# The slot lists of a mixture-of-experts router: loops written out, lanes dealt to three engines

## The chip, the cores and the metric

The kernel runs on one core of a Trainium2 chip. The metric is the device time of one execution in microseconds; the median of several executions is given. The profile is one more execution, taken with the hardware profiler.

## The reference

Input is `x` of shape (4, 2048, 256), so 8192 tokens of 256 numbers. One layer of causal attention with four heads is followed by a layer norm. Behind it stands a feed-forward layer with 32 experts and 16 adapters, and a second layer norm. Only the routing matters here:

```python
probs = softmax(h @ r2_w.T)                      # 8192 x 32
topp, topi = top_k(probs, 2)
wnorm = topp / topp.sum(-1, keepdims=True)       # the two gates of a token
score = where(routed, probs, -inf)
idx = argsort(-score, axis=0)[:cap].T            # cap = 320 tokens of each expert
w = take_along_axis(Wc.T, idx, 1) * valid        # their gates
```

Each expert works on at most 320 tokens. The kernel needs, for each expert and each of its slots, the token's number and its gate. The order of the slots within an expert is free, because the experts' outputs are added to the tokens' rows.

## The kernel before, in words

Four stages follow each other, each a block that ends with all engines meeting: `attention` (to about 1483 us of the span), `route` (to about 1786), `experts` (to about 2300) and `last_norm`.

In `route`, the 8192 tokens stand as 64 columns of 128 partitions. TensorE makes the logits, VectorE finds the two best experts of every token, searches each expert's threshold bit by bit (line 1214), and computes for each of the 64 x 2 pairs (token column, choice) the destination: a slot number from 0 to 12287, split into `dest_hi` (the slot's column, 0 to 95, since 32 experts have 3 columns of 128 slots each) and `dest_lo` (its lane, 0 to 127). Line 1274 releases the part that the change rewrites.

**The list stage** turns destinations into lists with matmuls. For each of the 128 pairs, `lane_hot` is a 128 x 128 matrix that has a 1 where the destination's lane is the column, and `col_hot` is a 128 x 192 matrix: 96 columns with the token's number plus 1 where the destination's column matches, and 96 with the gate there. The product of the two, added up over all 128 pairs in PSUM bank `ps[0]`, is the list: a slot that no pair hit stays 0. The pairs go in 16 lots of 8 (`LOT`, `LOTS`, lines 924 and 925), with two buffers, in a loop that handles two lots a turn:

- GpSimd (lines 1039 to 1051) waits until lot b - 2 is listed and ScalarE is through with it, copies the lot's 8 lane numbers to `lane_at` (1043), and makes the even lanes with a comparison (1046), four a lot.
- ScalarE (1069 to 1083) waits for that copy and makes the odd lanes, four a lot, each as an Abs (1076), a drain and a Relu (1078) of 1 - |distance|.
- VectorE (1277 to 1297) compares the column numbers for all 8 pairs at once (1282, 768 columns), drains, waits until lot b - 2 is listed, and multiplies by the token numbers (1289) and by the gates (1291).
- TensorE (1117 to 1135) waits for the columns of the lot, then for each lane in turn, and multiplies (1124). Its last matmul of the lot raises `listed`.

The buffers' release is what orders the engines: each of the three makers waits for `listed`. After the last lot VectorE reads PSUM (1299, 1300, 1302) and writes `slot_token` (1304) and `slot_weight` (1300). The block ends, and `experts` starts: GpSimd copies a list (1403) and gathers rows by it (1406). The weights of the first two experts were loaded in `route` (line 1006). Lines 801, 668 and 1658 are of the attention and of the last norm; they stand in the rows as instructions of the same kinds.

The waits, as TensorE has them:

```python
            def lists(b, r, first=False, last=False):
                pe.wait_ge(col_ready, b + 1)
                for n in range(LOT):
                    if n % 2:
                        pe.wait_ge(lane_odd, ODD + LOT // 2 * b + n // 2 + 1)
                    else:
                        pe.wait_ge(lane_even, LOT // 2 * b + n // 2 + 1)
```

Of the kernel before, what the change touches and what calls it, by code (L numbers as in the profile page):

```python
# [914 lines left out]
def route(nc, dram, NTT, cap, slot_token, slot_weight, w_raw, w_loaded):  # L915
# [8 lines left out]
    LOT = 8  # L924
    LOTS = NTT * TOPK // LOT
    assert TG % 4 == 0 and NTT % 16 == 0 and N <= 4096

    with ExitStack() as ctx:  # L928
# [25 lines left out]
        lane_hot = sb("lane_hot", [P, 2, LOT, P])  # L954
        lane_off = sb("lane_off", [P, 2, P])
        lane_at = sb("lane_at", [P, 2, LOT])
        col_eq = sb("col_eq", [P, 2, LOT, COLS])
        col_hot = sb("col_hot", [P, 2, LOT, 2, COLS])
        unit = sb("unit", [P, 1])
# [25 lines left out]
        dest_ready, lane_copied, lane_even, lane_odd = sem("dest_ready"), sem("lane_copied"), sem("lane_even"), sem("lane_odd")  # L985
        col_ready, listed = sem("col_ready"), sem("listed")

        LISTED, ODD = 2, LOT // 2 + 1

        def at(tensor, n, width=1):  # L990
            return tensor[:].rearrange("p a b c -> p (a b c)")[:, bass.ds(n, width)]
# [17 lines left out]
        def _(pool):  # L1009
# [24 lines left out]
            pool.sem_inc(lane_copied, ONE)  # L1034


            wait(pool, dest_ready, 1, pool_passed)

            def lanes(b, r):

                wait(pool, listed, LISTED + b - 1, pool_passed)
                wait(pool, lane_odd, ODD + (LOT // 2) * (b - 1), pool_passed)
                pool.tensor_copy(lane_at[:, r], at(dest_lo, LOT * b, LOT)).then_inc(lane_copied, 1)  # L1043
                wait(pool, lane_copied, ONE + b + 1, pool_passed)
                for n in range(0, LOT, 2):
                    pool.tensor_scalar(lane_hot[:, r, n, :], iota_p[:], lane_at[:, r, n:n + 1], None, ALU.is_equal)\
                        .then_inc(lane_even, 1)

            with pool.Fori(0, LOTS // 2) as j:
                for r in range(2):  # L1050
                    lanes(2 * j + r, r)
# [4 lines left out]
        def _(act):  # L1056
# [7 lines left out]
            act.sem_inc(lane_odd, ODD)  # L1064
# [4 lines left out]
            def lanes(b, r):  # L1069
                act.wait_ge(lane_copied, ONE + b + 1)  # L1070

                act.wait_ge(listed, LISTED + b - 1)
                for n in range(1, LOT, 2):

                    h = n // 2 % 2
                    act.activation(lane_off[:, h], iota_p[:], ACT.Abs, scale=-1.0, bias=lane_at[:, r, n:n + 1])  # L1076
                    act.drain()
                    act.activation(lane_hot[:, r, n, :], lane_off[:, h], ACT.Relu, scale=-1.0, bias=unit[:])\
                       .then_inc(lane_odd, 1)

            with act.Fori(0, LOTS // 2) as j:
                for r in range(2):
                    lanes(2 * j + r, r)

        @block.tensor
        def _(pe):
# [30 lines left out]
            def lists(b, r, first=False, last=False):  # L1117
                pe.wait_ge(col_ready, b + 1)
                for n in range(LOT):
                    if n % 2:  # L1120
                        pe.wait_ge(lane_odd, ODD + LOT // 2 * b + n // 2 + 1)
                    else:
                        pe.wait_ge(lane_even, LOT // 2 * b + n // 2 + 1)
                    mm = pe.matmul(ps[0][:, 0:2 * COLS], lane_hot[:, r, n, :], col_hot[:, r, n].rearrange("p a b -> p (a b)"),
                                   start=first and n == 0, stop=last and n == LOT - 1, skip_group_check=True)
                mm.then_inc(listed, 1)

            pe.sem_inc(listed, LISTED)
            lists(0, 0, first=True)
            lists(1, 1)  # L1130
            with pe.Fori(1, LOTS // 2 - 1) as j:
                for r in range(2):
                    lists(2 * j + r, r)
# [619 lines left out]
```

## Time and profile before

| | |
|---|---|
| median of 3 runs | 2359.52 us (2355.16 to 2361.84) |
| the profiled execution | 2361.54 us, its span 2359.6 us |
| mean granted clock of TensorE | 0.922 of full |
| TensorE matmul, busy | 1971.2 us (84%) |
| VectorE, busy | 1491.6 us (63%) |
| ScalarE, busy | 1331.8 us (56%) |
| GpSimd, busy | 823.7 us (35%) |
| GpSimd's lanes (line 1046), 64 of them | 64.7 us, 1028 ns each |
| from the start of line 1282 to that of line 1299 | 1712.14 to 1785.02 us |

How to read it: PE is TensorE's matmul, PEld its weight load, DVE VectorE, ACT ScalarE, POOL GpSimd. Times in the rows are microseconds from the span's start, unless ns is said. A float32 matmul is recorded as two weight loads and two matmuls. PEclk, in the table by stretches, is the granted clock, 1.0 being 2.4 GHz and 0.5 being 1.2 GHz. A timeline's row merges neighbouring instructions of one line and says how many (x4).

### The profile page before, as it was taken

To read this page: it belongs to the slowest core of one execution; us is meant where nothing else is said; L and a number is where in the kernel's file an instruction comes from. 1 tells how busy PE (TensorE), PEld (TensorE's weight loads), DVE (VectorE), ACT (ScalarE), POOL (GpSimd) and SP (SyncE) were. 2 spreads that over 40 slices of the span, in tenths; PEclk is the share of its full clock that TensorE was granted. 3 is DMA by queue.
4 is the path that set the end of the run, shared out by engine and by line. 5 is a ranking of instruction groups with operands and counts; after the bars stand their busy time and mean duration, and the time that the engine had idled before them with its cause. 6 is when DMAs were issued, how large, how long until landed. Compare 5 with 4: busy or idle time off the path is not lost. (4 is left out here: it accounts for less than half of the span.)

```text
span 2359.6 us, 43734 instructions
## 1 busy us (share of the span) xinstructions
PE 1971.2 (84%) x14340; PEld 1794.1 (76%) x14340; DVE 1491.6 (63%) x3318; ACT 1331.8 (56%) x3381; POOL 823.7 (35%) x937
## 2 busy tenths in 40 slices
PE   5799999999999999999999987501176999999990
PEld 5699988888988888988888876500155999999990
DVE  6655566656566656666666775288864666666655
ACT  4666665666665666665666653200065666666655
POOL 1122333333333333333111110000095666766652
PEclk9999999999999999999999998555598999999995
DMA  1000011001001001000000110300002444454428
GB/s 60 27 10 21 21 30 32 24 28 33 21 30 32 24 28 32 22 30 28 23 26 24 32 32 21 147 0 0 0 0 83 149 143 134 149 167 150 149 52 285
DMA packets 91405, 135.81 MB, mean 58 GB/s; under 512 B 16932, under 2 KB 79376, under 8 KB 87148
## 3 DMA queue, kind: packets, MB, share of 16 engines
q1 hardware_dynamic: 75372, 123.52, 15.2%
q0 software_dynamic: 15872, 10.24, 2.6%
q8 instruction: 90, 1.47, 0.3%
q14 instruction: 71, 0.58, 0.1%
HBM read 104.62 MB, written 39.85 MB: 61 GB/s over the span
## 5 line engine op out<-in xcount | busy, mean ns | idle before, releaser
L474 PE MATMUL out_ps<-v_sb,probs_t 128*128 128x64 f32 x4352 | 551.0, 271 | 17.6 <-DVE attn L773 15.1
L474 PEld LDWEIGHTS out_ps<-v_sb,probs_t 128*128 128x128 f32 x4352 | 532.4, 194 | 27.4 <-DVE probs_t L750 20.6
L736 DVE TENSOR_REDUCE part_max<-scores_ps 128x1 f32<-128x512 f32 (+3 forms) x576 | 356.9, 621 | 205.0 <-PE scores_ps L439 148.8
L611 ACT ACTIVATE probs<-scores_ps,neg_max 128x512 f32<-128x512 f32 (+3 forms) x640 | 398.1, 627 | 45.0 <-DVE neg_max L740 42.7
L439 PE MATMUL scores_ps<-k_st,q_parts 128*128 128x512 f32 (+3 forms) x1280 | 410.8, 403 | 11.4 <-ACT probs L611 5.0
L456 PE MATMUL probs_t_ps<-ident,probs 128*128 128x128 f32 x2176 | 347.6, 275 | 1.0 <-DVE probs_t L750 1.0
L620 ACT COPY probs_t<-probs_t_ps 128x512 f32<-128x512 f32 (+3 forms) x416 | 208.5, 501 | 244.6 <-PE probs_t_ps L456 243.2
L456 PEld LDWEIGHTS probs_t_ps<-ident,probs 128*128 128x128 f32 x2176 | 261.4, 142 | 51.4 <-issue 2.6
L1463 PE MATMUL up_ps<-xe_t,w 128*128 128x320 f32 x1920 | 288.9, 310 | 2.4 <-DVE xe_t L1570 1.7
L1463 PEld LDWEIGHTS up_ps<-xe_t,w 128*128 128x128 f32 x1920 | 283.6, 189 | 3.0 <-issue 1.9
L439 PEld LDWEIGHTS scores_ps<-k_st,q_parts 128*128 128x128 f32 x1280 | 200.5, 193 | 25.2 <-ACT probs L611 7.2
L879 POOL TENSOR_TENSOR rstd<-mean_var,power 128x1 f32<-128x1 f32 x64 | 35.6, 556 | 481.8 <-DVE mean_var L793 481.8
L898 POOL TENSOR_TENSOR products<-qk,cos_sin 128x256 f32<-128x256 f32 x176 | 125.4, 745 | 218.3 <-ACT qk L552 218.3
L1584 DVE SCALAR_TENSOR_TENSOR h<-silu,up_ps 128x320 f32<-128x320 f32 x160 | 77.1, 482 | 182.7 <-ACT silu L1540 182.7
L1426 POOL DMA_INDIRECT acc_rows<-out_rows,token x96 | 148.2, 1544 | 127.1 <-ACT out_rows L1553 116.1
L1463 PE MATMUL y_ps<-w,h_parts 128*128 128x256 f32 x1440 | 181.0, 285 | 0.0
L1463 PEld LDWEIGHTS y_ps<-w,h_parts 128*128 128x128 f32 x1440 | 174.4, 191 | 2.2
L1565 DVE TENSOR_TENSOR w<-w_raw,w 128x768 fp32r<-128x768 f32 x160 | 153.0, 958 | 5.0 <-ACT w L1518 0.7
L1406 POOL DMA_INDIRECT rows<-x_rows,token_in x96 | 129.8, 1352 | 48.3 <-POOL token_in L1403 27.5
L750 DVE COPY probs_t<-probs_t_ps 128x512 f32<-128x512 f32 (+1 forms) x224 | 145.9, 651 | 0.4 <-PE probs_t_ps L456 0.3
L1076 ACT ACTIVATE lane_off<-iota_p,lane_at 128x128 f32<-128x128 f32 x64 | 24.9, 390 | 206.6 <-POOL lane_at L1043 206.5
L1518 ACT CAST w<-w_raw 128x768 fp32r<-128x768 f32 x160 | 131.8, 826 | 2.0 <-PEq L928 2.0
(214 smaller groups left out, 3153.8 us busy)
## 6 DMA issues: line engine op xcount, KB each, us to landing
w_raw<-in_w_expert SPq DMA_DIRECT2D x32, 1536.0 KB, 6.4
w_raw<-in_w_adapter SPq DMA_DIRECT2D x32, 384.0 KB, 6.9
x_t<-in_x_t SPq DMA_DIRECT2D x64, 128.0 KB, 2.1
x_row<-in_x SPq DMA_DIRECT2D x64, 128.0 KB, 2.0
x_rows<-x SPq DMA_DIRECT2D x64, 128.0 KB, 1.7
acc_rows<-x SPq DMA_DIRECT2D x64, 128.0 KB, 1.8
ln_x<-acc_rows SPq DMA_DIRECT2D x16, 512.0 KB, 6.2
out_rows_dram<-ln_y SPq DMA_DIRECT2D x16, 512.0 KB, 5.2
```

What stands on the lines that cost most here:

```text
L439: mm = pe.matmul(out, q_parts[:, m % 2, part_, h, :], k_st[:, h, key_cols(g)], start=part_ == 0, stop=part_ == 1 and not diagonal)
L456: mm = pe.transpose(t_ps[:, g % 2, a:a + P], probs[:, g % PROBS_RING, a:a + P], ident[:])
L474: mm = pe.matmul(o_ps[:, h, :], probs_t[:, g % PT_RING, a - lo:a - lo + P], v_sb[:, slot(b, a // P), h, :], start=a == 0, stop=a == t * P)
L611: act.activation(probs[:, g % PROBS_RING, 0:hi - lo], s_ps[:, g % AHEAD, 0:hi - lo], ACT.Exp, bias=neg_max[:, u % 8:u % 8 + 1], accum_out= ...
L620: act.copy(probs_t[:, g % PT_RING, 0:hi - lo], t_ps[:, g % 2, 0:hi - lo]).then_inc(probs_copied[1], 1)
L736: red = dve.tensor_reduce(neg_max[:, ring:ring + 1] if single else part_max[:, ring, c:c + 1], s_ps[:, g % AHEAD, 0:hi - lo], AX.X, ALU.ma ...
L750: dve.tensor_copy(probs_t[:, g % PT_RING, 0:hi - lo], t_ps[:, g % 2, 0:hi - lo])\
L1406: pool.indirect_dma_start(out=rows[0:n, r, t, :], out_offset=None, in_=dram["x1"], in_offset=bass.IndirectOffsetOnAxis(ap=token_in[0:n, r, ...
L1426: pool.indirect_dma_start(out=dram["acc"], out_offset=bass.IndirectOffsetOnAxis(ap=token[0:n, r, t:t + 1], axis=0), in_=out[0:n, r, t, :], ...
L1463: mm = pe.matmul(o, left(a), right(b), start=start and n == 0, stop=stop and n == 2)
L1518: act.copy(columns(w[:, r, 0], p), columns(w_raw[:, r], p)).then_inc(w_upper, 1)
L1565: dve.tensor_tensor(columns(w[:, r, 1], p), columns(w_raw[:, r], p), columns(raw(w[:, r, 0]), p), ALU.subtract).then_inc(w_split, 1)
```

## The change

The list stage is written out lot by lot instead of looped. The eight lanes of a lot are dealt in a new way: two to GpSimd, three to ScalarE, three to VectorE. A lane now carries the token's number plus 1 instead of a 1: GpSimd and VectorE compare and multiply in one instruction, ScalarE's Relu computes token - token x |distance|. The column matrix is the bare mask and mask times gate, so one multiply falls away, and the comparison writes `col_hot` itself. GpSimd and ScalarE read `dest_lo` directly, so `lane_at` and its copy go. There are three buffers instead of two. TensorE takes VectorE's lanes first, then ScalarE's, then GpSimd's. The list's second half now sums token times gate, so at the end it is divided by the token number (by 1 where the slot is empty).

```diff
--- before.py
+++ after.py
@@ -922,6 +922,8 @@
     COLS = E * SL
     BITS = 30
     LOT = 8
+    LOT_RING = 3
+    POOL_LANES, ACT_LANES, DVE_LANES = (0, 3), (2, 5, 7), (1, 4, 6)
     LOTS = NTT * TOPK // LOT
     assert TG % 4 == 0 and NTT % 16 == 0 and N <= 4096
 
@@ -951,12 +953,11 @@
         same_e = sb("same_e", [P, P])
         before_g = sb("before_g", [P, P])
 
-        lane_hot = sb("lane_hot", [P, 2, LOT, P])
+        lane_hot = sb("lane_hot", [P, LOT_RING, LOT, P])
         lane_off = sb("lane_off", [P, 2, P])
-        lane_at = sb("lane_at", [P, 2, LOT])
-        col_eq = sb("col_eq", [P, 2, LOT, COLS])
-        col_hot = sb("col_hot", [P, 2, LOT, 2, COLS])
-        unit = sb("unit", [P, 1])
+        col_hot = sb("col_hot", [P, LOT_RING, LOT, 2, COLS])
+        token_neg = sb("token_neg", one)
+        tok_one = sb("tok_one", [P, COLS])
         hpre = sb("hpre", [P, NTT * P])
         key_b = sb("key_b", [P, N], BF16)
         passed_b = sb("passed_b", [P, N], BF16)
@@ -982,13 +983,14 @@
         key_ready, key_turned, key_copied = sem("key_ready"), sem("key_turned"), sem("key_copied")
         counted, summed = sem("counted"), sem("summed")
         slots_ready, slots_turned = sem("slots_ready"), sem("slots_turned")
-        dest_ready, lane_copied, lane_even, lane_odd = sem("dest_ready"), sem("lane_copied"), sem("lane_even"), sem("lane_odd")
+        dest_ready, lane_pool, lane_act = sem("dest_ready"), sem("lane_pool"), sem("lane_act")
         col_ready, listed = sem("col_ready"), sem("listed")
 
-        LISTED, ODD = 2, LOT // 2 + 1
-
-        def at(tensor, n, width=1):
-            return tensor[:].rearrange("p a b c -> p (a b c)")[:, bass.ds(n, width)]
+        def at(tensor, n):
+            return tensor[:].rearrange("p a b c -> p (a b c)")[:, n:n + 1]
+
+        def token_of(tensor, n):
+            return tensor[:].rearrange("p a b -> p (a b)")[:, n // TOPK:n // TOPK + 1]
 
         pool_passed, sp_passed = sem("pool_passed_b"), sem("sp_passed_b")
         block = ctx.enter_context(nc.Block())
@@ -1031,24 +1033,14 @@
                     pool.affine_select(out=m[:], in_=m[:], compare_op=ALU.not_equal, fill=1.0, base=-d * E,
                                        pattern=[[1, P]], channel_multiplier=-1).then_inc(cleared, 1)
                     n += 1
-            pool.sem_inc(lane_copied, ONE)
-
-
-            wait(pool, dest_ready, 1, pool_passed)
-
-            def lanes(b, r):
-
-                wait(pool, listed, LISTED + b - 1, pool_passed)
-                wait(pool, lane_odd, ODD + (LOT // 2) * (b - 1), pool_passed)
-                pool.tensor_copy(lane_at[:, r], at(dest_lo, LOT * b, LOT)).then_inc(lane_copied, 1)
-                wait(pool, lane_copied, ONE + b + 1, pool_passed)
-                for n in range(0, LOT, 2):
-                    pool.tensor_scalar(lane_hot[:, r, n, :], iota_p[:], lane_at[:, r, n:n + 1], None, ALU.is_equal)\
-                        .then_inc(lane_even, 1)
-
-            with pool.Fori(0, LOTS // 2) as j:
-                for r in range(2):
-                    lanes(2 * j + r, r)
+            pool.wait_ge(dest_ready, 1)
+            for b in range(LOTS):
+                r = b % LOT_RING
+                if b >= LOT_RING:
+                    pool.wait_ge(listed, b - LOT_RING + 1)
+                for n in POOL_LANES:
+                    pool.tensor_scalar(lane_hot[:, r, n, :], iota_p[:], at(dest_lo, LOT * b + n),
+                                       token_of(token1, LOT * b + n), ALU.is_equal, ALU.mult).then_inc(lane_pool, 1)
 
         CLEARED = 3 + (2 * G - 1) + (G - 1)
 
@@ -1061,26 +1053,22 @@
                 for g in range(G):
                     part = hpre[:, (g * TG + 4 * b) * P:(g * TG + 4 * b + 4) * P]
                     act.activation(part, part, ACT.Gelu, bias=b_r1[:]).then_inc(gelu_done, 1)
-            act.sem_inc(lane_odd, ODD)
             act.wait_ge(shifted, NTT // 16)
             flat = prob[:].rearrange("p a b c -> p (a b c)")
             act.activation(flat, flat, ACT.Exp).then_inc(exped, 1)
 
-            def lanes(b, r):
-                act.wait_ge(lane_copied, ONE + b + 1)
-
-                act.wait_ge(listed, LISTED + b - 1)
-                for n in range(1, LOT, 2):
-
-                    h = n // 2 % 2
-                    act.activation(lane_off[:, h], iota_p[:], ACT.Abs, scale=-1.0, bias=lane_at[:, r, n:n + 1])
+            act.wait_ge(dest_ready, 1)
+            for b in range(LOTS):
+                r = b % LOT_RING
+                if b >= LOT_RING:
+                    act.wait_ge(listed, b - LOT_RING + 1)
+                for n in ACT_LANES:
+                    h = len(ACT_LANES) * b + ACT_LANES.index(n)
+                    act.activation(lane_off[:, h % 2], iota_p[:], ACT.Abs, scale=-1.0, bias=at(dest_lo, LOT * b + n))
                     act.drain()
-                    act.activation(lane_hot[:, r, n, :], lane_off[:, h], ACT.Relu, scale=-1.0, bias=unit[:])\
-                       .then_inc(lane_odd, 1)
-
-            with act.Fori(0, LOTS // 2) as j:
-                for r in range(2):
-                    lanes(2 * j + r, r)
+                    act.activation(lane_hot[:, r, n, :], lane_off[:, h % 2], ACT.Relu,
+                                   scale=token_of(token_neg, LOT * b + n), bias=token_of(token1, LOT * b + n))\
+                       .then_inc(lane_act, 1)
 
         @block.tensor
         def _(pe):
@@ -1114,25 +1102,18 @@
                 mm = pe.transpose(ps[4 + j // 4][:, (j % 4) * P:(j % 4 + 1) * P], count[:, j * P:(j + 1) * P], ident[:])
             mm.then_inc(slots_turned, 1)
 
-            def lists(b, r, first=False, last=False):
+            for b in range(LOTS):
+                r = b % LOT_RING
                 pe.wait_ge(col_ready, b + 1)
-                for n in range(LOT):
-                    if n % 2:
-                        pe.wait_ge(lane_odd, ODD + LOT // 2 * b + n // 2 + 1)
-                    else:
-                        pe.wait_ge(lane_even, LOT // 2 * b + n // 2 + 1)
+                for n in DVE_LANES + ACT_LANES + POOL_LANES:
+                    if n in POOL_LANES:
+                        pe.wait_ge(lane_pool, len(POOL_LANES) * b + POOL_LANES.index(n) + 1)
+                    elif n in ACT_LANES:
+                        pe.wait_ge(lane_act, len(ACT_LANES) * b + ACT_LANES.index(n) + 1)
                     mm = pe.matmul(ps[0][:, 0:2 * COLS], lane_hot[:, r, n, :], col_hot[:, r, n].rearrange("p a b -> p (a b)"),
-                                   start=first and n == 0, stop=last and n == LOT - 1, skip_group_check=True)
+                                   start=b == 0 and n == DVE_LANES[0], stop=b == LOTS - 1 and n == POOL_LANES[-1],
+                                   skip_group_check=True)
                 mm.then_inc(listed, 1)
-
-            pe.sem_inc(listed, LISTED)
-            lists(0, 0, first=True)
-            lists(1, 1)
-            with pe.Fori(1, LOTS // 2 - 1) as j:
-                for r in range(2):
-                    lists(2 * j + r, r)
-            lists(LOTS - 2, 0)
-            lists(LOTS - 1, 1, last=True)
 
         @block.vector
         def _(dve):
@@ -1202,7 +1183,7 @@
                 dve.tensor_copy(key_t[:, c * 512:(c + 1) * 512], ps[4 + c][:])
             dve.drain()
             dve.tensor_copy(key_b[:], key_t[:].bitcast(BF16).rearrange("p (n a) -> p n a", a=2)[:, :, 1])
-            dve.memset(unit[:], 1.0)
+            dve.tensor_scalar(token_neg[:], token1[:], -1.0, None, ALU.mult)
             dve.memset(raw(cnt_r[:, 1:2]), 0.0)
             dve.wait_ge(cleared, CLEARED)
             dve.drain()
@@ -1274,34 +1255,29 @@
             dve.tensor_copy(dest_lo[:], lo_i[:]).then_inc(dest_ready, 1)
             dve.drain()
 
-            def columns(b, r):
-
-                full_lot = [P, LOT // TOPK, TOPK, COLS]
-                eq = col_eq[:, r].rearrange("p (q k) c -> p q k c", k=TOPK)
+            for b in range(LOTS):
+                r = b % LOT_RING
+                if b >= LOT_RING:
+                    dve.wait_ge(listed, b - LOT_RING + 1)
+                his, gates = (x[:].rearrange("p a b c -> p (a b c)")[:, LOT * b:LOT * (b + 1)].unsqueeze(2)
+                              .to_broadcast([P, LOT, COLS]) for x in (dest_hi, gate))
                 cols = iota_c[:].unsqueeze(1).to_broadcast([P, LOT, COLS])
-                dve.tensor_tensor(col_eq[:, r], cols, at(dest_hi, LOT * b, LOT).unsqueeze(2).to_broadcast([P, LOT, COLS]),
-                                  ALU.is_equal)
+                dve.tensor_tensor(col_hot[:, r, :, 0, :], cols, his, ALU.is_equal)
+                for n in DVE_LANES:
+                    dve.tensor_scalar(lane_hot[:, r, n, :], iota_p[:], at(dest_lo, LOT * b + n),
+                                      token_of(token1, LOT * b + n), ALU.is_equal, ALU.mult)
                 dve.drain()
-
-                dve.wait_ge(listed, LISTED + b - 1)
-                q = LOT // TOPK
-                tok = token1[:].rearrange("p a b -> p (a b)")[:, bass.ds(q * b, q)]
-                dve.tensor_tensor(col_hot[:, r, :, 0, :].rearrange("p (q k) c -> p q k c", k=TOPK), eq,
-                                  tok.unsqueeze(2).unsqueeze(3).to_broadcast(full_lot), ALU.mult)
-                dve.tensor_tensor(col_hot[:, r, :, 1, :], col_eq[:, r],
-                                  at(gate, LOT * b, LOT).unsqueeze(2).to_broadcast([P, LOT, COLS]), ALU.mult)\
-                   .then_inc(col_ready, 1)
-
-            with dve.Fori(0, LOTS // 2) as j:
-                for r in range(2):
-                    columns(2 * j + r, r)
-            dve.wait_ge(listed, LISTED + LOTS)
+                dve.tensor_tensor(col_hot[:, r, :, 1, :], col_hot[:, r, :, 0, :], gates, ALU.mult).then_inc(col_ready, 1)
+            dve.wait_ge(listed, LOTS)
             dve.tensor_scalar(empty[:], ps[0][:, 0:COLS], 0.0, DROPPED, ALU.is_equal, ALU.mult)
-            dve.tensor_copy(slot_weight[:].rearrange("p a b -> p (a b)"), ps[0][:, COLS:2 * COLS])
+            dve.tensor_scalar(tok_one[:], ps[0][:, 0:COLS], 1.0, None, ALU.max)
             dve.drain()
             dve.scalar_tensor_tensor(tok_f[:], ps[0][:, 0:COLS], -1.0, empty[:], ALU.add, ALU.add)
             dve.drain()
             dve.tensor_copy(slot_token[:].rearrange("p a b -> p (a b)"), tok_f[:])
+            dve.reciprocal(tok_one[:], tok_one[:])
+            dve.drain()
+            dve.tensor_tensor(slot_weight[:].rearrange("p a b -> p (a b)"), ps[0][:, COLS:2 * COLS], tok_one[:], ALU.mult)
 
 
 UP = 2 * 2 * INTER
```

## Rows read from the trace of the kernel before

**Rows 1.** The table by stretches: the list stage and the clock's rise.

```profile
core 0: us, PE busy (x) PEld busy (x) DVE busy (x) ACT busy (x) POOL busy (x), PEclk, DMA share, GB/s
1712.00:1785.00 73.00, 55.26 (x256) 43.00 (x256) 44.91 (x48) 46.13 (x128) 67.97 (x80) 0.93 0.00 0
1721.00:1722.00 1.00, 1.00 (x6) 1.00 (x6) 0.25 (x1) 0.86 (x3) 1.00 (x3) 0.70 0.05 16
1722.00:1724.00 2.00, 2.00 (x14) 1.96 (x13) 2.00 (x3) 1.78 (x6) 1.80 (x3) 1.00 0.00 0
```

**Rows 2.** The waits of the list stage: waiter, releaser, us in total, times, longest.

```profile
PE route_ps L1124 <- POOL lane_hot L1046: 29.1, 15, 17.1
PEld route_ps L1124 <- POOL lane_hot L1046: 25.2, 38, 1.5
DVE col_hot L1289 <- PE route_ps L1124: 22.2, 13, 2.5
PEld route_ps L1124 <- DVE col_hot L1291: 17.4, 1, 17.4
```

**Rows 3.** The timeline of GpSimd over one steady lot: start us, us, instruction.

```profile
1772.64 0.19 POOL L1043 COPY lane_at<-dest_lo 128x8 f32 x1
1773.03 4.05 POOL L1046 TENSOR_SCALAR lane_hot<-iota_p,lane_at 128x128 f32<-128x128 f32 x4 [0.20 <-POOL lane_at L1043]
...
1774.18 1.85 POOL L1046 TENSOR_SCALAR lane_hot<-iota_p,lane_at 128x128 f32<-128x128 f32 x1
1776.02 1.06 POOL L1046 TENSOR_SCALAR lane_hot<-iota_p,lane_at 128x128 f32<-128x128 f32 x1
1777.03 0.18 POOL L1043 COPY lane_at<-dest_lo 128x8 f32 x1
```

**Rows 4.** Durations of GpSimd's lanes, line L1046: ns min/median/max.

```profile
L1046 POOL TENSOR_SCALAR lane_hot<-iota_p,lane_at x64: 596/603/2223, 1713.4 to 1783.1; 128x128 f32<-128x128 f32 x64
```

**Rows 5.** The timeline of VectorE: the first lot, then a steady one.

```profile
1712.14 0.96 DVE L1282 TENSOR_TENSOR col_eq<-iota_c,dest_hi 128x768 f32<-128x768 f32 x1 [0.30 <-issue]
1715.11 1.04 DVE L1282 TENSOR_TENSOR col_eq<-iota_c,dest_hi 128x768 f32<-128x768 f32 x1
...
1773.81 0.98 DVE L1289 TENSOR_TENSOR col_hot<-col_eq,token 128x768 f32<-128x768 f32 x1 [1.58 <-PE route_ps L1124]
1774.71 0.95 DVE L1291 TENSOR_TENSOR col_hot<-col_eq,gate 128x768 f32<-128x768 f32 x1
1775.58 1.04 DVE L1282 TENSOR_TENSOR col_eq<-iota_c,dest_hi 128x768 f32<-128x768 f32 x1
```

**Rows 6.** The timeline of ScalarE's first lanes, and two of its lines at 256 columns.

```profile
1713.26 0.40 ACT L1076 ACTIVATE lane_off<-iota_p,lane_at 128x128 f32<-128x128 f32 x1 [186.08 <-POOL lane_at L1043]
1714.04 0.38 ACT L1076 ACTIVATE lane_off<-iota_p,lane_at 128x128 f32<-128x128 f32 x1
...
L1658 ACT ACTIVATE ln_y<-ln_x,ln_shift,ln_rstd x64: 583/585/601, 2314.7 to 2355.7; 128x256 f32<-128x256 f32 x64
...
L668 ACT ACTIVATE absolute<-x x64: 398/407/466, 171.3 to 1475.3; 128x256 f32<-128x256 f32 x64
```

**Rows 7.** The timeline of TensorE: the first matmuls, and weight loads without a wait.

```profile
1715.74 8.51 PE L1124 MATMUL route_ps<-col_hot,lane_hot 128*128 128x192 f32 x32 [17.06 <-POOL lane_hot L1046]
...
1782.06 2.62 PEld L1124 LDWEIGHTS route_ps<-col_hot,lane_hot 128*128 128x128 f32 x16 [0.31 <-issue]
```

**Rows 8.** Durations of VectorE's tensor_scalars with two pointers, lines L801 and L1241.

```profile
L801 DVE TENSOR_SCALAR x<-y,mean_var,rstd x64: 403/412/1421, 167.6 to 1474.5; 128x256 f32<-128x256 f32 x64
...
L1241 DVE TENSOR_SCALAR count<-count,offset,need x1: 1345/1345/1345, 1680.8 to 1680.8; 128x2048 f32<-128x2048 f32 x1
```

**Rows 9.** The timeline of VectorE's tail, and the reciprocal of line L1160.

```profile
1785.02 0.26 DVE L1299 TENSOR_SCALAR empty<-route_ps 128x96 f32<-128x96 f32 x1 [4.97 <-PE route_ps L1124]
1785.85 0.21 DVE L1304 CAST slot_token<-tok_f 128x96 int32<-128x96 f32 x1
...
L1160 DVE RECIPROCAL total<-total x1: 553/553/553, 1529.6 to 1529.6; 128x64 f32<-128x64 f32 x1
```


## The prediction

> **What bounds the kernel now.** The table by stretches comes first: the list stage, from the end of the destinations to the last matmul, lasts 73 us of the 2359.6 us span, GpSimd is busy for 68.0 of them and TensorE, VectorE and ScalarE for 55, 45 and 46 [rows 1]. The waits of that stage then say who is late: TensorE and its weight loads wait for GpSimd's lanes (29.1 and 25.2 us; 17 us of the first is the wait for the stage to begin), and VectorE waits 22.2 us for TensorE to free a buffer [rows 2]. Nobody in these rows waits for ScalarE, and for VectorE's columns only once. So GpSimd sets the pace. In steady state one of its lots is a copy at 1772.64, four lanes from 1773.03 and the next copy at 1777.03: 4.39 us a lot [rows 3], and 16 lots of that are 70 of the 73 us.
>
> Why four lanes take 4.05 us can be read there too. A lane alone takes 0.60 us, but the maximum is 2.22 [rows 4]. The third lane of the lot starts at 1774.18 and takes 1.85, the fourth at 1776.02 takes 1.06 [rows 3]. Meanwhile VectorE runs two back-to-back multiplies from 1773.81 to 1775.66 and its comparison to 1776.62 [rows 5]. A lane that starts behind a VectorE tensor_tensor does its 0.6 us only when that has ended; in return the tensor_tensor behind which it slips in takes 1.04 instead of 0.96 us [rows 5]. Of the 4.39 us, 2.4 are lane work, 1.7 are such waiting, the rest copy and semaphores. The end of this stage is waited for by everything: VectorE's last four instructions, the block's end, and only then the experts. What the stage loses or gains goes to the span in full.
>
> **Removed.** GpSimd: the copy of each lot and its wait (0.39 us a lot, 1772.64 to 1773.03 [rows 3]) and two of four lanes. VectorE: one of three 768-column instructions. ScalarE: one of four lanes. Loop branches and register instructions go too; they hide behind the waits for GpSimd now, so I count nothing for them.
>
> **GpSimd after.** Two lanes a lot. The lane now has two operations and two pointer scalars, and no row shows that form on GpSimd. Lower bound 0.60 us (the second operation is free), upper 1.2 (it costs as much again) [rows 4]; nothing makes it faster than the plain form. I take 0.60, the nearest row. Per lot there are two VectorE gaps at which a lane got in before (after the comparison, and between a multiply and the next comparison), so each lane pays one wait of 0.46 (1.06 less 0.60 [rows 3]): 2.1 us a lot. With 1.2 us a lane it is 3.3 us.
>
> **ScalarE after.** Three lanes. A lane takes 0.77 us from Abs to Abs (1713.26 to 1714.04 [rows 6]). Relu gets its scale from a pointer too: two pointers cost 583 less 398 ns for the same 256 columns, so one costs 0.09 us [rows 6]. 3 x 0.86 = 2.6 us a lot.
>
> **TensorE after.** The same 128 matmuls. 16 weight loads without a wait, a lot, take 2.62 us at the full clock (granted 1.0, 2.4 GHz) [rows 7]. The stage begins at the lower level (0.5, 1.2 GHz); in this trace the mean of 0.70 from 1721 to 1722 puts its rise at about 1721.6, 5.9 us after the first matmul at 1715.74 [rows 1, 7]. At half clock a lot is 5.2 us.
>
> **VectorE after.** One lot is: comparison 0.87 us start to start, three lanes, drain, multiply 0.87 [rows 5]. A lane is a tensor_scalar with two pointers: 256 columns take 0.403 us at best and 2048 take 1.345 [rows 8], so 0.526 ns a column, and 128 columns take 0.336 us. Neighbours overlap by 0.08 (0.95 us long, 0.87 apart), so lanes are 0.26 apart, together 0.78; then the last one's overlap 0.08 and the drain's gap, which I take as 0.08. Sum 2.68 us. Two GpSimd lanes slip in and cost 0.09 each: 2.86 us. That is under the 3.0 us that the old lots took where nothing held them (1712.14 to 1715.11 [rows 5]), and it is now the longest of the four. So the bound moves from GpSimd at 4.39 to VectorE at 2.86, with TensorE and ScalarE at 2.6 close behind; three buffers are what lets lots of nearly equal engines run without waiting for each other, and I cost their own waits at nothing because the first buffer is needed again only after three lots of VectorE (8.6 us), while TensorE's slow first lot is done by 1720.2.
>
> **The sum for the stage.** VectorE starts at 1712.14 and has written lot 15 at 1712.14 + 16 x 2.86 = 1757.9; TensorE, which is ready then, adds 2.62 and about 0.2 for the handovers: 1760.7. Check by TensorE: first columns at 1714.9, lot 0 at half clock to 1720.1, clock up at about 1720.8, lot 1 done at 1723.1, 14 more at 2.62 give 1759.8. The stage ended at 1785.0 [rows 9], so 24.3 us go.
>
> **Added.** At the tail, a reciprocal of 96 columns, a drain and a product behind the cast. The trace has a reciprocal of 64 columns at 0.55 us [rows 9]; 96 take between that and 0.83 in proportion, and I take 0.80. The tail is now 1.04 us (1785.02 to 1786.06 [rows 9]): 0.97 to the reciprocal's start, 0.80, 0.07, 0.24 make 2.08, so +1.0. The table of negative token numbers replaces a memset and lies on VectorE's path: +0.1. GpSimd and ScalarE now wait for the destinations instead of GpSimd's copy, which gives their first lanes 0.9 us that TensorE doesn't need. The experts, their gathers and weights are as before: they only start earlier.
>
> Together 24.3 - 1.1 = 23.2 us less. The profiled execution took 2361.54 us (span 2359.6), which gives 2338.3; it was 2.0 above the median 2359.52 of the three runs, against which it is 2336.3. I forecast 2337. 0.3%, 7.1 us, is about what a measurement of this kernel can tell from no change.
>
> **Rival 1, VectorE and GpSimd take turns.** VectorE's new lanes are tensor_scalars, and those are hurt by GpSimd in another way than its tensor_tensors: the same 256-column instruction takes 0.403 us at best and up to 1.421 [rows 8], a loss of up to 1.0, where a tensor_tensor lost 0.09. If a VectorE lane waits for a whole GpSimd lane, once a lot: 2.68 + 0.6 = 3.28, end at 1712.1 + 52.5 + 2.6 = 1767.2, 16.7 us gained, 2343. If twice: 3.88, end at 1776.8, 7.1 us gained, 2352. Against it: a GpSimd lane that begins under the multiply is over before the comparison behind it ends (0.6 against 0.87 us), and the VectorE lanes are short. The Trainium skill ("SBUF — State Buffer", Who interferes with whom) says that a VectorE instruction in a two-port mode and a GpSimd instruction exclude each other for the whole instruction, and the same for one with two SBUF inputs. By that rule it is the case of once or twice a lot; the trace agrees for GpSimd's side, not for the tensor_tensor, which lost only 0.09. Chance 0.24.
>
> **Rival 2, GpSimd starves and nothing is gained.** VectorE now has hardly a gap. If each lane waits as the longest one did (2.22 us [rows 4]), two lanes are 4.4 us a lot, the pace of now: 1712.4 + 71.0 + 0.6 = 1784.0, and the tail takes the rest, 2359.5. Against it: once VectorE is three lots ahead it stops and leaves GpSimd the port. Chance 0.07.
>
> **Rival 3, slower: GpSimd's lane with two operations.** Place: GpSimd's two lanes, which TensorE takes last. With a lane of 1.2 us plus the longest waiting seen (1.62), 16 lots are 90.2 us, the end 1803.2, and with the tail the kernel is 19.3 us slower: 2379. It decides from the point where a lane passes (1785.0 - 1.1 - 0.6 - 1712.4) / 32 = 2.2 us on average. Chance 0.05.
>
> **How the numbers follow.** Forecast 0.64. The low end is TensorE's own sum, another 0.9 us, with the executions' spread of some 4 us under the median: 2331. The high end takes in GpSimd at 3.3 us a lot (1765.8, 2341) and the first and most of the second case of rival 1: 2351. Faster by over 0.3%: 0.64 + 0.23 of rival 1 = 0.87; within: 0.08; slower: 0.05.
>
> **What would show it.** Right: the list stage 48 to 50 us long; VectorE busy nearly all of it, its lanes at 0.34 us; GpSimd's lanes 0.6 to 1.1 us; TensorE waiting mostly for VectorE's columns; the tail 2.1 us. Wrong: VectorE's lanes at 0.9 us (rival 1), TensorE waiting for GpSimd's lanes at over 1.5 us each (rivals 2 and 3), a clock that is still 0.5 after 1723, or a change in the experts' stage.

## The result, and the profile after

| | before | after |
|---|---|---|
| median | 2360.68 us (4 runs) | 2337.72 us (4 runs, 2336.17 to 2341.56) |
| the profiled execution | 2361.54 us, span 2359.6 | 2336.17 us, span 2334.3 |
| list stage, first comparison to VectorE's first instruction behind it | 72.88 us | 46.77 us |
| tail, from there to the last of `slot_token` and `slot_weight` | 1.04 us | 2.04 us |

The ratio is 0.9905, 95% interval 0.9885 to 0.9925: 23 us less.

The table by stretches first, for the same stage as in [rows 1], now 46.4 us, and around the clock's rise:

```profile
1711.20:1757.60 46.40, 43.90 (x256) 43.40 (x256) 42.31 (x80) 37.82 (x96) 44.17 (x32) 0.93 0.00 1
1716.00:1717.00 1.00, 1.00 (x4) 1.00 (x4) 1.00 (x2) 0.93 (x4) 1.00 (x1) 0.50 0.00 0
1717.00:1718.00 1.00, 1.00 (x6) 1.00 (x6) 1.00 (x4) 0.93 (x3) 1.00 (x2) 0.72 0.07 16
1718.00:1719.00 1.00, 1.00 (x8) 1.00 (x7) 0.93 (x2) 0.87 (x3) 1.00 (x2) 1.00 0.00 0
```

All of TensorE, VectorE, ScalarE and GpSimd are busy for 38 to 44 of 46.4 us; before, only GpSimd was. The waits of the stage answer to [rows 2]:

```profile
PEld route_ps L1113 <- DVE col_hot L1270: 16.5, 2, 16.3
PE route_ps L1113 <- DVE col_hot L1270: 16.1, 1, 16.1
DVE empty L1272 <- PE route_ps L1113: 3.0, 1, 3.0
```

TensorE's waits for GpSimd are gone (of the 29.1 us in [rows 2], 17.1 were the wait for the stage to begin, 12 were lost inside it). Of its 16.5 us of waiting for VectorE 16.3 are the wait for the stage's first columns, and nobody waits for a buffer. The timeline of TensorE's weight loads shows how little waiting is left:

```profile
1713.70 40.89 PEld L1113 LDWEIGHTS route_ps<-col_hot,lane_hot 128*128 128x128 f32 x240 [16.30 <-DVE col_hot L1270]
1754.76 2.57 PEld L1113 LDWEIGHTS route_ps<-col_hot,lane_hot 128*128 128x128 f32 x16 [0.17 <-DVE col_hot L1270]
```

From its first lot on TensorE waits 0.2 us in all (16.5 less 16.3), for its last two lots. So VectorE and TensorE are level here: TensorE starts late, spends its first 3.9 us at the lower clock, and catches up with VectorE only at the end. Now the timeline of VectorE, which answers to [rows 5] (the rows of three neighbouring lots, then of the last one and the tail, [rows 9]):

```profile
1710.89 0.96 DVE L1265 TENSOR_TENSOR col_hot<-iota_c,dest_hi 128x768 f32<-128x768 f32 x1
...
1715.42 0.97 DVE L1270 TENSOR_TENSOR col_hot<-col_hot,gate 128x768 f32<-128x768 f32 x1
1716.31 0.95 DVE L1265 TENSOR_TENSOR col_hot<-iota_c,dest_hi 128x768 f32<-128x768 f32 x1
1717.18 0.90 DVE L1267 TENSOR_SCALAR lane_hot<-iota_p,dest_lo,token 128x128 f32<-128x128 f32 x3
1718.16 0.97 DVE L1270 TENSOR_TENSOR col_hot<-col_hot,gate 128x768 f32<-128x768 f32 x1
1719.05 0.95 DVE L1265 TENSOR_TENSOR col_hot<-iota_c,dest_hi 128x768 f32<-128x768 f32 x1
...
1751.89 0.95 DVE L1265 TENSOR_TENSOR col_hot<-iota_c,dest_hi 128x768 f32<-128x768 f32 x1
1753.74 0.97 DVE L1270 TENSOR_TENSOR col_hot<-col_hot,gate 128x768 f32<-128x768 f32 x1
1757.66 0.26 DVE L1272 TENSOR_SCALAR empty<-route_ps 128x96 f32<-128x96 f32 x1 [2.96 <-PE route_ps L1113]
1758.49 0.21 DVE L1277 CAST slot_token<-tok_f 128x96 int32<-128x96 f32 x1
1758.62 0.75 DVE L1278 RECIPROCAL tok_one<-tok_one 128x96 f32<-128x96 f32 x1
1759.44 0.26 DVE L1280 TENSOR_TENSOR slot_weight<-route_ps,tok_one 128x96 f32<-128x96 f32 x1
```

VectorE runs without a gap: the comparison at 1716.31, three lanes from 1717.18, the multiply at 1718.16, the next comparison at 1719.05. That is 2.74 us a lot, and 1710.89 to 1751.89 is 15 lots in 41.0 us, 2.73 each. Its instructions end the stage: TensorE's last lot begins behind the multiply of 1753.74, and VectorE then waits 2.96 us for it. Now GpSimd's lanes by their line, ns min/median/max:

```profile
L1042 POOL TENSOR_SCALAR lane_hot<-iota_p,dest_lo,token x32: 836/1498/2343, 1710.9 to 1754.2; 128x128 f32<-128x128 f32 x32
```

VectorE's lanes by their line, in the same form:

```profile
L1267 DVE TENSOR_SCALAR lane_hot<-iota_p,dest_lo,token x48: 333/390/431, 1711.8 to 1753.3; 128x128 f32<-128x128 f32 x48
```

And the timeline of GpSimd, first one lane of a lot, then the next:

```profile
1715.91 1.93 POOL L1042 TENSOR_SCALAR lane_hot<-iota_p,dest_lo,token 128x128 f32<-128x128 f32 x1
```

```profile
1717.83 0.84 POOL L1042 TENSOR_SCALAR lane_hot<-iota_p,dest_lo,token 128x128 f32<-128x128 f32 x1
```

GpSimd's two lanes of a lot take 1.93 and 0.84 us, together 2.77, just VectorE's lot. The one that starts at 1715.91, under the multiply, waits for it and for the comparison behind it, which ends at 1717.26, and is done at 1717.84; the next runs from 1717.83 to 1718.67, under the last of VectorE's lanes, the drain and the first half of the multiply, and loses next to nothing. GpSimd is therefore "busy" all the time (44 of 46 us) and yet bounds nothing: much of that is waiting inside the instruction.

### The profile page after: what moved, and what is told of

Read it like the earlier page. It is cut to its first block and busy times, and to the rows that moved or that the text cites. A ratio compares the mean times of both kernels' runs of the same rounds, so it can differ in the third digit from the quotient of the medians.

```text
span 2334.3 us, 43294 instructions
## 1 busy us (share of the span) xinstructions
PE 1958.8 (84%) x14340; PEld 1793.7 (77%) x14340; DVE 1491.7 (64%) x3352; ACT 1324.2 (57%) x3349; POOL 801.7 (34%) x889
## 5 line engine op out<-in xcount | busy, mean ns | idle before, releaser
L439 PE MATMUL scores_ps<-k_st,q_parts 128*128 128x512 f32 (+3 forms) x1280 | 410.2, 402 | 11.2 <-ACT probs L611 5.1
L439 PEld LDWEIGHTS scores_ps<-k_st,q_parts 128*128 128x128 f32 x1280 | 200.6, 193 | 25.1 <-ACT probs L611 7.2
L611 ACT ACTIVATION_READ_ACCUMULATOR probs<-scores_ps,neg_max 128x1 f32 x640 | 130.3, 204 | 0.0
```

Of the source, the lines that this page charges most:

```text
L439: mm = pe.matmul(out, q_parts[:, m % 2, part_, h, :], k_st[:, h, key_cols(g)], start=part_ == 0, stop=part_ == 1 and not diagonal)
L611: act.activation(probs[:, g % PROBS_RING, 0:hi - lo], s_ps[:, g % AHEAD, 0:hi - lo], ACT.Exp, bias=neg_max[:, u % 8:u % 8 + 1], accum_out= ...
```

## The experiments

Each kernel's stage length is read from its own profile, as in the table above; the stage is the part that the change touches, and it began anywhere from 1709.1 to 1715.9 us in these profiles, also where nothing ahead of it differed. That scatter is why the whole times are less sharp than the stage. Each stage rests on one profile. "A lot" is the distance of two comparisons of VectorE in steady state: 4.39 us before, 2.74 after. All lots of the changed kernel are of that length but for the first of 2.68; in the other kernels the first lots, while buffers are still free or the clock is low, can differ.

**1. Only written out.** The kernel before, with its four loops unrolled:

```diff
-            with pool.Fori(0, LOTS // 2) as j:
-                for r in range(2):
-                    lanes(2 * j + r, r)
+            for b in range(LOTS):
+                lanes(b, b % 2)
```

and the same on the three other engines.

> The kernel before with its lots written out and nothing else. Theory (GpSimd's four lanes a lot set the pace, 4.39 us): the list stage, from the first comparison to VectorE's first instruction behind it, stays at 70 to 73 us (72.9 before, 46.8 after), the time at 2357 to 2361. Rival (the loops' branches and register instructions carried much of the gain): stage 60 us or less, time 2348 or less.

Measured: stage 70.40 us, 4.28 a lot, median 2357.63, ratio 0.9987 (0.9975 to 1.0000). Writing out is worth 2.5 us of 26.1, within the theory's range.

**2. The old deal in the changed kernel.**

```diff
-    POOL_LANES, ACT_LANES, DVE_LANES = (0, 3), (2, 5, 7), (1, 4, 6)
+    POOL_LANES, ACT_LANES, DVE_LANES = (0, 2, 4, 6), (1, 3, 5, 7), ()
```

TensorE takes the lanes in the old order 0 to 7 again, so this experiment undoes the deal and TensorE's order together.

> The changed kernel with the old deal of lanes: GpSimd four, ScalarE four, VectorE none, in TensorE's old order. Three buffers, written-out lots, direct reading and lanes that carry the token stay. Theory (the deal is what gained): GpSimd needs four lanes of 0.84 us and one or two waits behind VectorE, 4.2 to 4.9 us a lot, stage 68 to 79 us, time 2358 to 2368, no better than before. Rival (the third buffer and the missing copy gained): 3.4 us a lot or less, stage 56 us or less, time 2347 or less.

Measured: stage 63.58 us, 3.80 a lot, median 2353.48, ratio 0.9961 (0.9947 to 0.9975). Between the two theories: the deal, with TensorE's order, is the largest part (16.8 us), but something else had gained 7 us over kernel 1. GpSimd is still the one waited for. Its lanes by their line, then the waits of the stage:

```profile
L1042 POOL TENSOR_SCALAR lane_hot<-iota_p,dest_lo,token x64: 784/787/1924, 1715.9 to 1777.7; 128x128 f32<-128x128 f32 x64
```

```profile
DVE col_hot L1265 <- PE route_ps L1113: 22.2, 13, 2.2
PEld route_ps L1113 <- POOL lane_hot L1042: 14.8, 31, 0.8
PE route_ps L1113 <- POOL lane_hot L1042: 5.9, 27, 0.4
```

A lane with two operations takes 0.787 us when nothing is in its way, and four of them make 3.15 of the 3.80 us; only 0.65 us a lot is left of waiting for VectorE. In the kernel before that was 1.7.

**3. The old columns in the changed kernel.** Lanes of 0 or 1 on all three engines, and

```diff
-                dve.tensor_tensor(col_hot[:, r, :, 0, :], cols, his, ALU.is_equal)
+                dve.tensor_tensor(col_eq[:, r], cols, his, ALU.is_equal)
...
+                dve.tensor_tensor(col_hot[:, r, :, 0, :].rearrange("p (q k) c -> p q k c", k=TOPK),
+                                  col_eq[:, r].rearrange("p (q k) c -> p q k c", k=TOPK),
+                                  tok.unsqueeze(2).unsqueeze(3).to_broadcast(full_lot), ALU.mult)
```

> The changed kernel with the old columns: lanes are 0 or 1 again, VectorE multiplies the mask by the token number and by the gate (three instructions of 768 columns a lot), and the reciprocal at the end goes. Theory (VectorE's own work sets the pace at 2.74 us a lot): 0.87 more for the multiply, some 0.17 less for three lanes with one pointer less: 3.44 us a lot, stage 57 to 59 us, tail 1.0 shorter, time 2347 to 2350. Rival (TensorE at 2.57 us or GpSimd's lanes set it, VectorE has room): stage 50 us or less, time 2340 or less.

Measured: stage 57.99 us, 3.39 a lot, tail 1.03, median 2348.82, ratio 0.9944 (0.9927 to 0.9961). What VectorE gets to do more comes out at the end in full, so VectorE is a bound after the change. It does not follow that a faster VectorE would gain as much: TensorE has only 0.2 us to spare in the changed kernel. The waits of its stage:

```profile
PEld route_ps L1113 <- DVE col_hot L1276: 27.2, 13, 17.3
POOL lane_hot L1042 <- PE route_ps L1113: 13.0, 11, 1.7
ACT lane_off L1067 <- PE route_ps L1113: 12.2, 13, 2.3
```

TensorE waits for VectorE 13 times, and the two other makers wait for a buffer, so all three have time to spare.

**4. Two buffers instead of three** (`LOT_RING = 2`).

> The changed kernel with two buffers instead of three. Theory (with two buffers VectorE and TensorE still overlap fully, since a lot of each is about 2.7 us; only TensorE's slow first lot, at the lower clock, holds VectorE): stage 1 to 3 us longer, 48 to 50 us, time 2338 to 2341. Rival (engines of nearly equal pace need the third buffer, each handover costs): 0.5 us a lot, stage 54 us or more, time 2345 or more.

Measured: stage 51.24 us, 2.96 a lot, median 2339.73, ratio 0.9907 (0.9890 to 0.9923). The stage is 4.5 us longer, more than the theory said, less than the rival. The whole times of the two kernels, 2.0 us apart at the median, don't tell them apart; the stage does. Its timeline of VectorE, at the start and in steady state:

```profile
1713.62 0.97 DVE L1270 TENSOR_TENSOR col_hot<-col_hot,gate 128x768 f32<-128x768 f32 x1
1716.23 0.96 DVE L1265 TENSOR_TENSOR col_hot<-iota_c,dest_hi 128x768 f32<-128x768 f32 x1 [1.64 <-PE route_ps L1113]
...
1739.87 0.96 DVE L1265 TENSOR_TENSOR col_hot<-iota_c,dest_hi 128x768 f32<-128x768 f32 x1 [0.22 <-PE route_ps L1113]
1741.74 1.08 DVE L1270 TENSOR_TENSOR col_hot<-col_hot,gate 128x768 f32<-128x768 f32 x1
1742.74 0.95 DVE L1265 TENSOR_TENSOR col_hot<-iota_c,dest_hi 128x768 f32<-128x768 f32 x1
...
1745.78 0.96 DVE L1265 TENSOR_TENSOR col_hot<-iota_c,dest_hi 128x768 f32<-128x768 f32 x1 [0.22 <-PE route_ps L1113]
```

1.64 us are the slow first lot, as expected. The rest comes in pairs of lots: one of 2.87 us, whose multiply is stretched to 1.08 beside a lane of GpSimd (0.96 at most where GpSimd makes no lanes, experiment 7), and one of 3.04 with a wait for the buffer. My reading, argued and not tested: a second buffer that comes free just as it is needed passes each delay of one engine on to the other.

**5 and 6. One lane more, or one less, for GpSimd**, taken from or given to VectorE.

```diff
-    POOL_LANES, ACT_LANES, DVE_LANES = (0, 3), (2, 5, 7), (1, 4, 6)
+    POOL_LANES, ACT_LANES, DVE_LANES = (0, 3, 6), (2, 5, 7), (1, 4)
```

> One of VectorE's three lanes goes to GpSimd: GpSimd three, ScalarE three, VectorE two. Theory (GpSimd gets in twice in a lot of VectorE, so two lanes are its limit beside a VectorE without gaps): VectorE's lot would be 2.4 us, but GpSimd's three lanes need 3 us or more, TensorE waits for them; stage 50 to 60 us. Rival (GpSimd has room, each lane only stretches to the time it is given): TensorE sets the pace at 2.57, stage 44 to 46 us.

```diff
-    POOL_LANES, ACT_LANES, DVE_LANES = (0, 3), (2, 5, 7), (1, 4, 6)
+    POOL_LANES, ACT_LANES, DVE_LANES = (0,), (2, 5, 7), (1, 3, 4, 6)
```

> One of GpSimd's two lanes goes to VectorE: GpSimd one, ScalarE three, VectorE four. Theory (VectorE sets the pace, a lane costs it 0.29 to 0.33 us start to start): 3.0 to 3.1 us a lot, stage 51 to 53 us. Rival (VectorE's lanes are stretched by GpSimd's, fewer of those free it): a lot stays within 2.8 us, stage 48 us or less.

Measured, one execution each: stages 61.07 us (3.85 a lot) and 50.29 us (2.93 a lot), times 2351.33 and 2337.88. With three lanes GpSimd is the bound again, 1 us beyond the range given for it: TensorE waits for it and VectorE waits for buffers, in the waits of its stage:

```profile
PEld route_ps L1113 <- POOL lane_hot L1042: 14.9, 22, 1.2
DVE col_hot L1265 <- PE route_ps L1113: 13.7, 11, 1.3
```

With one lane VectorE's lot grows by 0.19 us, less than the theory's 0.26 or more, and the stage stays 0.7 us under the range given; the likely cause is that its four lanes are 0.342 us at the median instead of 0.390. Both neighbours of the deal are longer in the stage; the whole time, 2337.88 us beside a median of 2337.72, doesn't tell one lane from two.

**7. No lanes on GpSimd at all.** GpSimd's lanes and TensorE's matmuls with them are left out, a quarter of the pairs.

```diff
-                for n in DVE_LANES + ACT_LANES + POOL_LANES:
+                for n in DVE_LANES + ACT_LANES:
```

and GpSimd's loop is removed.

> GpSimd makes no lanes and TensorE leaves out the two matmuls of each lot that use them, so a quarter of the pairs is missing from the lists and their slots stay empty; all else as changed. It measures what GpSimd's presence costs VectorE, whose pace sets the stage. Theory (GpSimd costs VectorE's lanes little): a VectorE lane falls from 0.39 us (median beside GpSimd) to 0.33, a lot from 2.74 to 2.68 us or less, stage 44 to 46 us. Rival 1 of the prediction (a VectorE lane waits for a GpSimd lane): a lot falls to 2.4 us or less.

Measured, one execution: stage 45.17 us, 2.67 a lot, time 2336.89. VectorE's lanes by their line, to be compared with 333/390/431 above:

```profile
L1257 DVE TENSOR_SCALAR lane_hot<-iota_p,dest_lo,token x48: 339/341/345, 1715.4 to 1756.0; 128x128 f32<-128x128 f32 x48
```

GpSimd's presence costs VectorE 0.06 us a lot, 1 us in 16 lots. The other 0.6 us by which this stage is shorter is TensorE's last lot, which has six pairs here (VectorE waits 2.31 us for it instead of 2.96). With all eight pairs TensorE would take back most of the 1 us, as it has 0.2 us to spare. Rival 1 of the prediction is refuted: VectorE's lanes don't wait for GpSimd's.

**8 and 9. Where the other 7 us are.** The kernel of experiment 2 with two buffers (`LOT_RING = 2`), and the kernel of experiment 3 with the old deal and TensorE's old order (as in experiment 2).

> The old deal of lanes as in the run before it (GpSimd four, ScalarE four, VectorE none; stage 63.6 us there), and two buffers instead of three. It asks where the 7 us come from that the old deal still had over the written-out kernel (70.4 us). Theory (they come from GpSimd's shorter lot, and buffers are nothing while one engine is far slower than the rest): stage 63 to 65 us. Rival (the third buffer gave them): stage 68 us or more.

> The old deal and the old columns (three VectorE instructions a lot, lanes of 0 or 1 with one operation) with three buffers and direct reading of the destinations. Theory (without the copy and its handover GpSimd's lot is 4.4 less 0.4 us; its lanes are 0.60 instead of 0.79 us, but VectorE has a third instruction that they wait behind): 3.9 to 4.1 us a lot, stage 63 to 67 us. Rival (the multiply that went from VectorE gave the gain, not the copy): stage 69 to 72 us.

Measured: experiment 8 has a stage of 63.26 us (63.58 with three buffers), ratio 0.9969 (0.9954 to 0.9984). Beside a GpSimd that bounds, the third buffer is nothing. Experiment 9 has 69.59 us, 4.27 a lot, ratio 0.9994 (0.9981 to 1.0008): the rival holds. The copy and its handover, which I had priced at 0.4 us a lot, are, together with the third buffer, worth 0.8 us in all, and nothing in steady state (4.28 us a lot in experiment 1, 4.27 here). GpSimd's lanes by their line:

```profile
L1042 POOL TENSOR_SCALAR lane_hot<-iota_p,dest_lo x64: 593/828/2187, 1714.3 to 1781.7; 128x128 f32<-128x128 f32 x64
```

A lane takes 0.6 us at best and 1.06 in the mean (68.0 us busy for 64). The timelines of GpSimd show where the copy's time went: the two lanes of a steady lot that wait, in experiment 1 and then in experiment 9.

```profile
1753.50 1.85 POOL L1046 TENSOR_SCALAR lane_hot<-iota_p,lane_at 128x128 f32<-128x128 f32 x1
1755.34 1.06 POOL L1046 TENSOR_SCALAR lane_hot<-iota_p,lane_at 128x128 f32<-128x128 f32 x1
```

```profile
1757.48 1.30 POOL L1042 TENSOR_SCALAR lane_hot<-iota_p,dest_lo 128x128 f32<-128x128 f32 x1
1758.77 1.85 POOL L1042 TENSOR_SCALAR lane_hot<-iota_p,dest_lo 128x128 f32<-128x128 f32 x1
```

Less 0.6 us of work for each lane, 1.7 us of a lot are waiting behind VectorE with the copy, and 1.95 without it: what the missing copy gave back is spent waiting behind VectorE.

So the 26.1 us of the stage, along a chain of kernels (before, experiments 1, 9, 2, after): written out 2.5 (72.9 to 70.4), no copy and a third buffer 0.8 (to 69.6), one multiply less and the token in the lane 6.0 (to 63.6), the deal with TensorE's order 16.8 (to 46.8). Of the last, 12.0 come with two buffers (63.3 to 51.2), the third buffer adds 4.5, and 0.3 are what two buffers gain in the old deal. Taken in another order the parts would be others, and steps of less than 1 us rest on one profile each. TensorE's order was not tried by itself. Of the kernels that make the whole list none has a shorter stage than the changed one.

## Why the prediction was right

**The bound before, and that it moves from GpSimd to VectorE.** Shown for GpSimd: experiments 2, 5 and 8 hand it lanes back and it bounds again. For VectorE: experiment 3 hands it its multiply back and the stage grows by 11.2 us. But TensorE is level with it and not merely close behind: it waits 0.2 us in all after its first lot begins.

**VectorE's lot.** Forecast 2.68 us for its own work and 0.18 for two lanes of GpSimd slipping in, 2.86; experiment 7 measures 2.67 for the first, the changed kernel 2.74 for both. The term that was too large is the slipping in: 0.06 instead of 0.18. The tensor_tensors stay at 0.95 to 0.97 us, not 1.04, and GpSimd gets its turn during VectorE's lanes, which lengthen by 0.04 us each in the mean (0.382 beside 0.341). A lane of VectorE was forecast at 0.336 us from lines with two pointers, and is 0.341 without GpSimd.

**The stage.** Forecast 48.6 us (1712.14 to 1760.7), measured 46.77, which is also under the 48 to 50 us given as a sign. The difference is the 0.12 us a lot above, 16 times. It reaches the end of the stage only because TensorE's clock rose early as well (below).

**GpSimd's lane.** Taken at 0.60 us with the bound at 1.2; it is 0.787, so the second operation and pointer are not free. And each lane was to wait once behind VectorE for 0.46 us: in fact one waits 1.1 us and the other hardly at all, 2.77 us a lot instead of 2.1. My two gaps a lot were wrong: a lane did not get in between the multiply and the comparison that follows it. It cost nothing, as VectorE's lot is as long; that was luck, and the sign "GpSimd's lanes 0.6 to 1.1 us" did not come true. By my costs a third lane would have made 3.2 us a lot (3 x 1.06); experiment 5 has 3.85, and 14 us more for the stage.

**TensorE and ScalarE.** A lot of TensorE was forecast at 2.62 us, and is 2.57 in the profile after; ScalarE's second pointer was to cost 0.09 us: 493 ns beside 402. The clock was to rise 5.9 us after the first matmul and rose earlier: 0.72 granted from 1717 to 1718 puts it at 1717.6, 3.9 us after the first matmul at 1713.70. The forecast had no reason for an earlier rise, and it helped: 2.0 us more at the lower clock would have cost TensorE some 1.0 us, of which its 0.2 us of waiting covers little, so by this estimate the stage would have been some 0.8 us longer, set by TensorE.

**The loops.** Counted as nothing, because they "hide behind the waits for GpSimd". They don't quite: experiment 1 gains 2.5 us without them, 4.39 to 4.28 us a lot. The forecast did not need this term, since it builds the time after from VectorE's own lot.

**The buffers.** Their waits at nothing: right. With two, the cost would have been 4.5 us.

**The tail.** +1.0 forecast, 2.04 against 1.04 measured; the reciprocal is 0.75 us where I took 0.80. No run shows the 0.1 us for the table of negative token numbers by its effect on the time.

**The sum.** 23.2 us less forecast. The profiled executions are 25.4 apart, the medians 23.0. Stage and tail give 25.1 of the 25.4, and the rest nearly cancels: the stage began 1.25 us earlier, and what follows the tail took 1.1 us longer. So the mechanism gave 1.9 us more than I forecast, and that 2337 meets the median of 2337.72 so closely is in part luck with the spread of the executions.

**The rivals.** Rival 1 is refuted by experiment 7: of the 0.6 us that a VectorE lane would wait for a GpSimd lane, 0.06 a lot are seen in all. The exclusion that the Trainium skill states for a two-port VectorE instruction and a GpSimd instruction ("SBUF — State Buffer", Who interferes with whom) does not appear between these lanes: three VectorE lanes ran in 0.90 us (1717.18 to 1718.08) across the end of one GpSimd lane and the start of the next. But it does appear in this program between a VectorE tensor_scalar and a GpSimd tensor_tensor, and the 1.421 us from which I made the rival is such a case. From the timelines of both engines in the attention of the kernel before:

```profile
347.90 1.42 DVE L801 TENSOR_SCALAR x<-y,mean_var,rstd 128x256 f32<-128x256 f32 x1
347.89 1.27 POOL L858 TENSOR_TENSOR q_parts<-q_t,q_parts 128x512 fp32r<-128x512 f32 x1
```

The VectorE instruction takes 0.40 us alone, and ends here 0.16 us behind GpSimd's. All 20 instructions of this line that took over 0.45 us ran beside such a GpSimd tensor_tensor. So my rival took over a loss from a GpSimd tensor_tensor to a GpSimd tensor_scalar, where it does not hold. The other half of the rule, that a VectorE instruction with two SBUF inputs contends with GpSimd, agrees with the lane of 1.93 us, which waited; it agrees less with the lane of 0.84 us, half of which ran under a multiply that took 0.97 us instead of 0.96. Rival 2 did not come about: GpSimd's lanes do stretch, to 1.40 us on average (44.5 us for 32), but not to 2.2. Rival 3 falls with the 0.787 us.

## What to carry to other kernels

Deal work out until the engines' times per round are equal, and price the deal by what an engine can do beside its neighbour, not alone: here GpSimd makes 1.6 us of work in a round of 2.7 next to a busy VectorE, and a third lane takes the stage from 47 to 61 us. Look also for the engine that is level with the new bound: less work for VectorE alone would gain some 0.2 us here beyond an earlier first lot, an estimate from TensorE's remaining waits. An instruction taken from VectorE can be worth most to GpSimd, which waits behind it (6.0 us here, while VectorE itself bounded nothing). An extra buffer is worth nothing beside one slow engine and 4.5 us between equal ones, so test it in the balanced version.

## What the runs showed of the hardware

- GpSimd's tensor_scalar of 128 float columns takes 0.596 us with one operation and one pointer (the kernel before) and 0.787 with two of each (experiment 2); VectorE's takes 0.34 us for the latter and 0.27 at best for the former, as its line in experiment 3 shows:

```profile
L1270 DVE TENSOR_SCALAR lane_hot<-iota_p,dest_lo x48: 273/313/393, 1712.8 to 1764.7; 128x128 f32<-128x128 f32 x48
```

- A GpSimd lane that starts under a VectorE tensor_tensor waits for it and for another one directly behind it (1.93 us for 0.79 of work). A lane that starts just ahead of one loses 0.05 us at most (0.84). The VectorE tensor_tensor loses 0.01 to 0.12 us as a rule (0.97 in the changed kernel, 1.08 in experiment 4), and 0.2 once (1.165 us beside 0.958, in the kernel before).
- A VectorE tensor_scalar and a GpSimd tensor_tensor take turns (1.42 us for 0.40 of work), a VectorE tensor_scalar and a GpSimd tensor_scalar don't (0.382 us beside 0.341).
- VectorE's reciprocal takes 0.553 us for 64 columns and 0.75 for 96, some 6 ns a column, where a plain instruction takes 1 (0.26 us for 96 columns, 0.95 for 768).
- TensorE's clock rose 5.9 us (before), 3.9 us (after) and, with two buffers, 2.9 us after the first matmul of the stage (1711.9; the granted clock is the third figure from the end in this row of the table by stretches):

```profile
1714.00:1716.00 2.00, 2.00 (x11) 2.00 (x11) 0.59 (x1) 0.28 (x1) 1.25 (x2) 0.79 0.05 8
```
